# The order of work around a recurrent scan: three pauses added and one shortened in the first layer's side streams

## The reference, cut to what matters

```python
h = rms_norm(x, ln1_w); xx = shift(h) - h
r, k, v, g, w = (mix(h, xx, mu) @ W ...)          # five mixes of h and xx
S = decay * S + k v^T;  o = r (S_before + u k v^T)  # step by step over 2048 tokens
x = x + (group_norm(o) * silu(g)) @ Wo
x = x + gelu(rms_norm(x) @ ffn_w1) @ ffn_w2
x = x + shared experts + sum over experts of gate[t, e] * gelu(x @ up_e) @ down_e   # top 4 of 16 by softmax
```

## Time and profile before

| what | value |
|---|---|
| median of 3 runs | 4982.31 us (4976.38 to 4983.9) |
| the profiled execution's own time | 4976.51 us |
| its span in the trace | 4974.7 us |
| mean granted TensorE clock | 0.935 |
| busy over the span: PE, DVE, POOL, ACT | 88%, 77%, 61%, 51% |
| 13 steady chunks of the first layer, 286.5 to 2165.1 us | 1878.6 us |

### The profile page before, as it was taken

How to read it: one execution, slowest core, us unless ns; L and a number is a source line. 1 busy time by engine, 2 the same in 40 slices (tenths; PEclk the granted TensorE clock), 3 DMA queues, 4 the chain that set the end, 5 groups by cost and what they waited for, 6 DMA issues and landing times.

```text
span 4974.7 us, 58244 instructions
## 1 busy us (share of the span) xinstructions
PE 4357.1 (88%) x18832; PEld 2868.4 (58%) x18832; DVE 3827.0 (77%) x6152; ACT 2521.3 (51%) x4753; POOL 3045.1 (61%) x1956
## 2 busy tenths in 40 slices
PE   5789999999999999998988889998988888489994
PEld 1355555555555555565655655555555555378883
DVE  6897888878777887884168888888888888645677
ACT  1244333433433343333567777777777776245552
POOL 3455554545545455553167888888888888745552
PEclk7899999999999999999989999999999998699997
DMA  4233332333333233332121121112221111486787
GB/s 143 80 106 107 104 102 85 109 106 102 106 104 104 84 108 106 98 110 84 45 85 55 71 71 64 64 65 74 77 84 65 70 65 61 162 240 205 255 279 279
DMA packets 302509, 545.46 MB, mean 110 GB/s; under 512 B 30592, under 2 KB 146560, under 8 KB 293248
## 3 DMA queue, kind: packets, MB, share of 16 engines
q1 hardware_dynamic: 274560, 466.08, 29.0%
q0 software_dynamic: 27648, 75.67, 4.2%
HBM read 422.71 MB, written 118.92 MB: 109 GB/s over the span
## 4 chain that ended last, share of the span: by engine, by line
PE 59%; DVE 18%; ACT 10%; POOL 6%; issue 4%; DMA 2%; SPq 0%; DVEq 0%; another core or an unknown queue 0%; POOLq 0%; ACTq 0%
PE psum L207 23%; PE psum L783 8%; PE psum L1891 5%; DVE c_hs L1426 5%; PE psum L658 5%; POOL c_dbx L1408 4%; PE psum L1150 4%; PE psum L1442 3%; DVE a_S L885 3%; PE psum L1914 3%; PE psum L1198 3%; DVE a_prod L891 2%; PE psum L907 2%; ACT psum L1415 2%; PE psum L1876 1%
## 5 line engine op out<-in xcount | busy, mean ns | idle before, releaser
L1408 POOL TENSOR_TENSOR c_dbx<-c_dtx,c_Brep 128x1024 f32<-128x1024 f32 x512 | 1203.0, 2365 | 266.6 <-DVE c_hs L1426 211.3
L876 POOL TENSOR_TENSOR a_kv<-a_rk,a_kv 128x512 f32<-128x512 f32 x512 | 813.5, 1601 | 387.4 <-DMA a_kv<-v_rows 387.4
L1426 DVE TENSOR_TENSOR_SCAN c_hs<-psum,c_carry,c_dbx 128x512 f32<-128x512 f32 x768 | 934.8, 1264 | 148.7 <-ACT psum L1415 115.9
L802 POOL TENSOR_TENSOR a_hid_e<-a_hid_e,a_g_rep 128x512 f32<-128x512 f32 x256 | 386.8, 1513 | 823.8 <-ACT a_hid_e L791 646.9
L885 DVE TENSOR_TENSOR_SCAN a_S<-a_decay,a_carry,a_kv 128x513 f32<-128x513 f32 x512 | 792.0, 1547 | 103.0 <-POOL a_kv L876 99.0
L1415 ACT ACTIVATE psum<-c_dt,c_cols 128x512 f32<-128x512 f32 x1024 | 694.1, 687 | 296.7 <-DVE c_hs L1426 288.1
L1442 PE MATMUL psum<-ident,c_hs 128*128 128x128 f32 x4096 | 656.6, 299 | 152.8 <-DVE c_hs L1426 146.5
L1442 PEld LDWEIGHTS psum<-ident,c_hs 128*128 128x128 f32 x4096 | 521.7, 153 | 410.5 <-DVE c_hs L1426 239.8
L891 DVE TENSOR_TENSOR a_prod<-a_rk,a_S 128x512 f32<-128x512 f32 x512 | 580.9, 1135 | 78.8 <-PE psum L907 78.8
L783 PE MATMUL psum<-a_W_down,a_hid_e 128*128 128x256 f32 x2304 | 550.9, 385 | 62.1 <-DVE a_carry L883 35.5
L207 PE MATMUL psum<-a_xT,a_W_up 128*128 128x512 f32 x1152 | 561.1, 617 | 26.2 <-ACT a_hid_e L791 15.2
(11 more groups left out here) (263 smaller groups left out, 6890.9 us busy)
## 6 DMA issues: line engine op xcount, KB each, us to landing
a_kv<-v_rows SPq DMA_DIRECT2D x512, 256.0 KB
a_g_rep<-g_rows SPq DMA_DIRECT2D x256, 256.0 KB, 4.0
c_Brep<-b_rows SPq DMA_DIRECT2D x64, 1024.0 KB
d_xs<-sorted_rows SPq DMA_DIRECT2D x320, 128.5 KB
d_w<-results SPq DMA_DIRECT2D x64, 512.0 KB, 11.4
d_w<-in_d_experts SPq DMA_DIRECT2D x32, 768.0 KB
sorted_rows<-d_zeros SPq DMA_DIRECT2D x66, 128.5 KB, 11.3
a_xa<-in_L_attn_x SPq DMA_DIRECT2D x16, 512.0 KB, 4.6
```

The source lines that it names most:

```text
L876: m_kv[g] = pool.mark(nc.gpsimd.tensor_tensor(kv[:, g % NV, 1:C + 1], rk[slot][:, 1, hb, :], kv[:, g % NV, 1:C + 1], ALU.mult))
L1408: m_dbx[g] = m_dbx[g + 1] = pool.mark(nc.gpsimd.tensor_tensor(dbx[:, r:r + 2, :], dtx[slot][:, e, :].unsqueeze(1).broadcast_to([P, 2, C]), ...
L1426: m_scan[q] = dve.mark(nc.vector.tensor_tensor_scan(hs[:, q % NR, :], psum[:, DA + q % ND, :], dbx[:, q % NX, :], first, ALU.mult, ALU.add))
```

## The change

Each of the four edits is one pause. In `before`, the plain `yield` between `scaled` and `transposed` becomes `rest(1)`, and a `rest(2)` is put between the store of the value rows and the mix "mu_g". In `expert_inputs`, a `rest(1)` is put between the first three fetches of gates and the mark `("gates", c)`. In `experts_out`, `rest(2)` ahead of the last sums becomes `rest(1)`.

```diff
--- before.py
+++ after.py
@@ -410,7 +410,7 @@
             yield
             act.after(m, m_done.get(("mixed", c - 1)))
             m = m_done["xa free", c] = yield from scaled(ha, xa, roots[:, TL:], shift[0])
-            yield
+            yield from rest(1)
             act.after(m_halo)
             marks = yield from transposed(ha, lambda kb: hT[:, kb, 1:C + 1], m, lambda kb: cols["ln1_w"][:, kb:kb + 1])
             yield
@@ -505,6 +505,7 @@
             m_done["stored", c] = True
             if c == 0:
                 m_done["ready", c] = [m_k, m_r, m_decay]
+            yield from rest(2)
             buf, m_x = mixed(6, "mu_g")
             m_done["mixed", c] = m_x
             yield
@@ -808,7 +811,7 @@
 
             slot = c % 2
             xb_ = xb[slot]
-            yield from rest(2)
+            yield from rest(1)
             dve.after(m_down, m_done["read x", c])
             for half, (i, bank) in enumerate(banks):
                 part = flat(xb_[:, 2 * half:2 * half + 2, :])
```

## The result

The changed kernel takes 5091.4 us, the median of 4 runs (5083.99 to 5099.62); the kernel before, run beside it, takes 4983.1 (4976.38 to 4987.09, 4 runs). The ratio is 1.0221 with a 95% interval of 1.0208 to 1.0233. So it is 108 us slower, where 60 us faster was forecast, and it lies 86 us above the top of the range (5005). The profiled execution took 5099.62 us (span 5097.8, mean granted clock 0.925), 8.2 above the median.

The account below looks back on a forecast made before the run. PE bounds the kernel, idle 10.1 us a chunk; 2.4 + 0.5 + 2.0 - 0.6 + 1.2 - 0.5 = 5.0 won, 65 in 13; less 5 for the first chunk, -60: 4916.5, median 4922. Range 4875 to 5005.

Parts of the forecast that it names:

- kind A: Chunks where `before` starts with two moves: the transposition goes from s6 to s7, 3.7 us won there.
- Pause before the transposition: In `before`: PE's wait for ACT at the transposition shrinks, a mean of 2.4 us won in a chunk.
- For waits on banks that I can't see from the trace: -0.5: Allowance for unseen waits on banks: 0.5 us lost in a chunk, bounds 0 and -3.
- kind B: Chunks where `before` starts with one move: the transposition stays at s6, 1.1 us won there.
- Pause before "mu_g": DVE's mix in `before`: no cost on PE itself, but late pieces ahead of L815 lose 0.6 us a chunk.
- Pause at the gates: Before the gates' mark: PE's gated "down" waits less for POOL, 1.0 us every second chunk, mean 0.5 won.
- The slower rival: At s2 to s4 the gates come late and PE runs dry: +3 us a chunk, 5026 us; chance 0.21.
- Last sums: One step less before L815 at the boundary: 2.0 us won in a chunk, bounds -1 to 2.79.
- Clock: PE's low clock behind gaps: half of the 2.4 us lost in a chunk comes back, 1.2 won.
- The gaps did move: Rival: the transposition gains 2.4 us and the boundary loses as much through a later L815, 4978 us; chance 0.17.
- DVE's ports: Rival: POOL's k-v product slows two DVE scans at the boundary by 1.0 us each, 26 us, 4948; chance 0.10.
- The first chunk: Its own term, with the "mu_g" mix now inside it: 5 us taken, between +1 and +10.

Follow-up runs that it names:

- slip only: Kernel before, with only `attention_out` waiting one step more before its products with Wo (L590): 5065.04 us, ratio 1.0156.
- the fastest version: Kernel before plus the gates' and last sums' edits, with all four L359 written at once before the transposition: 4927.86 us, ratio 0.9886.
- mix, same rhythm: Kernel before plus only the "mu_g" pause, with `before`'s leftover fraction of a move set to 1.0 at each chunk's start: 5038.49 us, ratio 1.0109.
- rhythm only: Kernel before with no edit, but `before`'s leftover fraction of a move set to 0.6 at each chunk's start: 5190.33 us, ratio 1.0417.

## Why the prediction was wrong

**What bounds the kernel: right.** PE was the bound and DVE had room; "mu_g"'s 91.7 us of waiting on DVE vanished and were worth nothing. The four places of idle time were real, and three of them lost their wait; the first "down" kept 25.1 of 34.8 us. Two of the signs given for being wrong came true: chunks over 146 us (153 in the mean), and a first "down" that still waits, mostly 3.24 us behind a chunk of kind A.

**Pause before the transposition, "mean 2.4" won a chunk: wrong in sign.** Alone it costs 96 us, 7.6 a chunk in the 13 chunks (1977.7 against 1878.6). My text has the cause in one sentence, "the second L590 and L604 slip by a step, the feed-forward starts and ends a step later", and then costs it at nothing but a later gate. The term for it was "For waits on banks that I can't see from the trace: -0.5". This is the step that failed: the slip alone measures 79 us, 6.1 for each of 13 chunks (5.6 by the windows, where the chunks take 1951.2 instead of 1878.6), twelve times the value I took and twice my outer bound of -3. I had taken one step of 4.5 us as the most that it could cost, as if a late stream lost only its own time. What the slip does is to leave PE without written work while ACT goes through another stream's logarithm and its two table loads: `attention_out`'s in kind A (4.22 us), the group norm's at the feed-forward there and in "slip only" (3.44 us). Behind such gaps the clock is halved for a while. For kind B my text was nearly right at the place itself (2.91 us left, 2.6 forecast); what it lacks is the wait of 3.47 us for L464, whose products came to stand right behind it.

**Pause before "mu_g", "at nothing on PE": wrong.** Alone +89. I counted what comes to stand ahead of L815 (-0.6), and that was about its size: with the same rhythm PE waits 11 us more there, 0.9 a chunk. I had also seen that `before` would end late and that chunks of two kinds would follow, but priced kind B's start only at the transposition, and the rhythm is some 34 of the 89. Of the other 55, the wait in `expert_inputs`' transposition (25.7 us) was not in my sum, nor the longer busy time (31.7 us), where I had the clock as a gain.

**Pause at the gates, +0.5: right in sign, too small.** Alone -30 us, 2.1 a chunk in the windows. I had its wait falling only in every second chunk; with no other edit it goes in nearly all (1.7 us left of 22.7), and DVE's wait at the scan, which I moved "to a later scan", mostly disappears (11.2 of 84.5). The slower rival, PE running dry for want of credit behind this pause, is refuted by the same run: it had the sign of the result and the wrong place. Its mark, the wait for L728, shows only with the transposition's pause alone, and is 7.6 us there.

**Last sums, +2.0: too large alone (-20 us, 1.1 a chunk in the windows), and not additive.** With the gates' edit nothing measurable is left of it (-31 together, -30 for the gates alone); beside the pauses of `before` the wait for L815 comes back (25.1 us in 12).

**Clock, +1.2 won: wrong in sign.** Lost were 4.0 us a chunk; the new gaps are longer (3.4 to 4.2 us) than those of before (1.2 to 3.1).

**The other rivals.** The gaps did move, but not to the boundary and not in equal measure. DVE's ports did not decide: DVE is busy 36 us less in the 13 chunks than before. In the runs of the gates' edit alone and of the fastest version DVE is busy 9.9 and 30 us longer over the span, and both are faster; a price of that kind, if it is the ports', is hidden behind PE. The first chunk was a small term, as forecast, but of the other sign: by the windows 5.1 us lost (112.0 against 106.9) where I took 5 won.

**The rival I lacked.** What I should have written is a rival: "a bank held a step longer makes `attention_out` slip, and PE runs out of written work while ACT has its logarithm and two table loads (1.28 us each, as L559's in the earlier trace rows) ahead of the next expert activation". It could have been priced from the trace of before, where ACT needs 4.87 us from L613's start at 906.96 to L791's at 911.83, and PE has 1.93 and 1.98 us of written work from 909.19 on. In the changed kernel the same row takes from 949.12 to 953.99, again 4.87 us; PE has its last written work done at 950.42 and stands idle for 4.22, to 954.64.

The Trainium skill ("ScalarE: Activation LUTs", "What ACT_TABLE_LOAD costs") prices a switch to another set of functions at about 2.66 us, 1.28 for the load and 1.38 for a drain. The load agrees with every row above; the drain is not seen, since the load of 952.69 starts as soon as L344 (952.47, 0.21 us) has ended and L794 starts at 953.99, 0.02 us after the load's end. By the Trainium skill two switches would be 5.3 us, and by the rows they are 2.6.

**Left open.** Why all four edits cost 27 us less than the sum of each alone; how the 55 us of "mix, same rhythm" divide between the late sums, the transposition and the clock behind each; how much of "rhythm only" is a matter of banks and how much of L470 standing right behind L464; that it is banks which carry the transposition's pause over to `attention_out` follows from the program's order and was not tested by a run with a bank more; whether the transposition's pause would win if `attention_out` were held in its steps, which was not tried.

## What to carry to other kernels

A pause in a hand-woven order need not be local: it can hold banks and end a stream later, and the cost is paid where another stream then slips. Before adding one, list for each neighbour the step in which it takes its banks, and price its slip by what would stand ahead of the next activation on ACT's in-order queue, table loads included, less the work that PE has written beside it. Here a wait between two instructions was removed more safely by writing its producer earlier within the same step, so that no later piece changes its step: that won 21 us where the pause lost 96.

## What the runs showed of the hardware

Nearly half of the loss is the clock. Over 13 chunks PE was idle 60.7 us longer and busy 52.0 longer, and the whole program has the same 18832 instructions; behind two gaps of 3.4 us the granted clock stood at 0.50 for the next 3.5 and 4.0 us. Behind the 2.79 us gap of before, eight matmuls took 3.10 instead of 1.89 us, so that gap cost 1.2 us more than itself. And ACT, busy 49% of the span, set PE's start in three places of a pair of chunks (3.47, 4.22 and 3.44 us): the busy share of an engine did not tell whether another one waits for it.
